# The expert stage's row loads issued from SyncE instead of ScalarE

## The reference

```python
x = x + tanh(g_xattn) * xattn(layernorm(x), ctx_512, ...)   # 16 heads, 375 context rows
x = x + tanh(g_ffn)   * ffn(layernorm(x), ...)

# ffn, N = 16 * 112 = 1792 tokens, E = 64 experts, H = 512, I = 128:
logits = x @ gate_w.T
topv, topi = top_k(logits, 8)
W = zeros((N, E)); W[n, topi[n]] = softmax(topv[n])
gate, up = split(einsum('nh,eih->nei', x, gu_w))
out = einsum('nei,ehi->nh', silu(gate) * up * W[:, :, None], dp_w)
out = out + sigmoid(x @ sh_gate1_w.T) * (silu(x @ sh_gate_w.T) * (x @ sh_up_w.T)) @ sh_down_w.T
```

## Time and profile before

| | |
|---|---|
| median of three runs | 1579.57 us |
| profiled execution, its time | 1578.49 us |
| profiled execution, span of the core | 1576.7 us |
| mean granted TensorE clock | 0.966 of full speed |
| busy: PE, PEld | 91%, 74% |
| busy: DVE, ACT, POOL | 72%, 43%, 50% |
| HBM traffic | 240 GB/s over the span |

### The profile page before, as it was taken

One profiled execution on the slowest core, in us unless ns is written; L12 is line 12 of the kernel. 1 busy time (PEld: TensorE's weight loads), 2 busy tenths in 40 slices (PEclk: granted clock), 3 DMA queues, 4 the chain that ended last, 5 costly groups with the idle time before them and its releaser, 6 DMA issues.

```text
span 1576.7 us, 24944 instructions
## 1 busy us (share of the span) xinstructions
PE 1430.7 (91%) x7674; PEld 1165.9 (74%) x7674; DVE 1140.1 (72%) x2601; ACT 671.6 (43%) x1558; POOL 784.4 (50%) x858
## 2 busy tenths in 40 slices
PE   6999799999899999989999999988299999999985
PEld 5766787777688777768777767867189999988742
DVE  5767684188788258779618887726388999988587
ACT  3332574011277011147501117703167777767521
POOL 4654573045577438777434787523524443333322
PEclk9999899999999999999999999998599999999998
DMA  7898993555596677730085764087799999999698
GB/s 243 293 318 280 288 299 95 194 170 182 179 285 203 218 242 245 231 103 17 28 274 185 234 195 149 3 287 247 220 311 331 330 359 370 369 339 348 203 429 343
DMA packets 164358, 380.08 MB, mean 241 GB/s; under 512 B 20200, under 2 KB 55682, under 8 KB 162434
## 3 DMA queue, kind: packets, MB, share of 16 engines
q1 hardware_dynamic: 136182, 286.33, 54.6%
q0 software_dynamic: 20608, 62.28, 11.5%
q10 hardware_dynamic: 7436, 29.88, 5.6%
HBM read 238.82 MB, written 139.59 MB: 240 GB/s over the span
## 4 chain that ended last, share of the span: by engine, by line
PE 60%; DVE 14%; DMA 11%; issue 7%; POOL 5%; ACT 2%; SPq 1%; POOLq 0%; DVEq 0%; ACTq 0%
PE bank L777 16%; PE bank L779 15%; PE bank L778 15%; PE bank L875 7%; PE bank L901 3%; DMA p_in<-parts 3%; DMA w_ex<-in_w_ex 3%; DVE q_sin L1190 2%; DMA parts<-y_sb,to_row 2%; PE bank L1040 2%; POOL q_rope L1846 2%; POOL slot_rows L1868 1%; DVE q_rope L1186 1%; POOL prob L1852 1%; DMA x_sb<-in_x 1%
## 5 line engine op out<-in xcount | busy, mean ns | idle before, releaser
L1846 POOL TENSOR_TENSOR q_rope<-q_rope,q_sin 128x448 f32<-128x448 f32 x192 | 217.7, 1162 | 157.6 <-DVE q_sin L1190 157.4
L1924 POOL DMA_INDIRECT parts<-y_sb,to_row x140 | 137.3, 981 | 220.7 <-ACT y_sb L1752 190.5
L1852 POOL TENSOR_TENSOR prob<-prob,row_inv 128x375 f32<-128x375 f32 x219 | 176.5, 812 | 103.6 <-DVE row_inv L1212 101.3
L875 PE MATMUL bank<-q_rope,m_w 128*128 128x448 f32 x384 | 159.7, 552 | 13.9 <-DVE q_tl L1196 10.4
L1190 DVE TENSOR_TENSOR q_sin<-bank,sin_q 128x448 f32<-128x448 f32 (+1 forms) x256 | 158.1, 617 | 4.0
L1868 POOL DMA_INDIRECT slot_rows<-rows,pos_i x112 | 110.0, 982 | 92.8 <-DVE count L1297 64.3
L1204 DVE TENSOR_REDUCE row_max<-bank 128x1 f32<-128x375 f32 x224 | 119.5, 534 | 39.7 <-PE bank L779 39.1
L901 PE MATMUL bank<-ident,prob 128*125 128x128 f32 x672 | 115.0, 282 | 21.8 <-POOL prob L1852 10.3
L1614 ACT ACTIVATE prob<-bank,row_max 128x375 f32<-128x375 f32 x224 | 128.3, 573 | 12.8 <-DVE row_max L1204 12.2
L901 PEld LDWEIGHTS bank<-ident,prob 128*125 128x125 f32 x672 | 103.3, 190 | 31.3 <-POOL prob L1852 20.9
L875 PEld LDWEIGHTS bank<-q_rope,m_w 128*128 128x128 f32 x384 | 71.9, 193 | 70.9 <-issue 65.9
(11 more groups left out here) (364 smaller groups left out, 4392.9 us busy)
## 6 DMA issues: line engine op xcount, KB each, us to landing
w_ex<-in_w_ex SPq DMA_DIRECT2D x64, 768.0 KB
slot_rows<-blank SPq DMA_DIRECT2D x64, 612.0 KB
p_in<-parts SPq DMA_DIRECT2D x14, 2048.0 KB, 16.8
m_w<-m_dram SPq DMA_DIRECT2D x48, 192.0 KB
x_g<-slot_rows ACTq DMA_DIRECT2D x16, 476.0 KB
wq_s0h<-wq_dram SPq DMA_DIRECT2D x24, 256.0 KB
wq_s0l<-wq_dram SPq DMA_DIRECT2D x24, 256.0 KB
wq_s1h<-wq_dram SPq DMA_DIRECT2D x24, 256.0 KB
```

The lines of the kernel that those rows point to most:

```text
L875: m = pe.matmul(bank[5][:, 0:GT], m_w[n % NW][:, c, :], q_rope[h % 2][:, c, :], start=(c == 0), stop=(c == QC - 1))
L1846: pool.tensor_tensor(o[:, c, :], o[:, c, :], q_sin[:, c, :], ALU.add).then_inc(s_radd, 1)
L1852: pool.tensor_tensor(prob[i][:], prob[i][:], row_inv[:, i:i + 1].to_broadcast([P, L]), ALU.mult)\
L1924: pool.indirect_dma_start(parts, bass.IndirectOffsetOnAxis(ap=to_row[x % NROW][0:size, t:t + 1], axis=0), y_sb[x % NY][t][0:size, :], None)\
```

## The change

`load_slots` moves from the shared helpers into `sync`, so that SP issues all 64 row loads. In SP's loop the row load for x + 5 stands ahead of the weight load for x + 3. ACT's loop has no row load any more, and ACT's wait for `s_order` in front of the stage goes as well; SP keeps its own.

```diff
-        def load_slots(eng, x):
-            e = eng.value_load(order[0:1, x:x + 1], min_val=0, max_val=E - 1)
-            size, n = TILES[x]
-            if x >= NXE:
-                eng.wait_ge(s_et, FIRST[x - NXE + 1])
-                eng.wait_ge(s_own, 3 * (x - NXE) + 1)
-            eng.dma_start(x_g[x % NXE][0:size, 0:n, :], ...).then_inc(s_xg[x % NXE], 16)
...
+            def load_slots(x):
+                e = sp.value_load(order[0:1, x:x + 1], min_val=0, max_val=E - 1)
+                size, n = TILES[x]
+                if x >= NXE:
+                    sp.wait_ge(s_et, FIRST[x - NXE + 1])
+                    sp.wait_ge(s_own, 3 * (x - NXE) + 1)
...
...
             for x in range(NXE):
-                load_slots(sp, x)
+                load_slots(x)
                 if 1 <= x + 1 < NE:
                     load_expert(x + 1)
             for x in range(E):
+                if x + NXE < E:
+                    load_slots(x + NXE)
                 if x + NE < E:
                     load_expert(x + NE)
                 if x in REST_AT:
                     load_base(EARLY_TILES + REST_AT.index(x))
...
             act.wait_ge(s_route, NR * B)
-            act.wait_ge(s_order, 1)
...
                 if x < E:
                     inner(x)
-                if x + NXE < E:
-                    load_slots(act, x + NXE)
                 if x >= 1:
                     down(x - 1)
```

More of the change, by code:

```diff
@@ L490, in behind_loop @@
                         body(eng, r, x)
-        def load_slots(eng, x):
-            e = eng.value_load(order[0:1, x:x + 1], min_val=0, max_val=E - 1)
-            size, n = TILES[x]
-            if x >= NXE:
-                eng.wait_ge(s_et, FIRST[x - NXE + 1])
-                eng.wait_ge(s_own, 3 * (x - NXE) + 1)
-            eng.dma_start(x_g[x % NXE][0:size, 0:n, :], slot_rows.rearrange("(e m) w -> e m w", m=SPAN)
-                         [bass.ds(e, 1), 0:size * n, :].rearrange("one (p t) w -> p (one t) w", t=n))\
-                .then_inc(s_xg[x % NXE], 16)
         def sync(sp):
@@ L730, in load_expert @@
                     .then_inc(s_ew[x % NE], 16)
+            def load_slots(x):
[4 more added lines that the diff above has]
+                    sp.wait_ge(s_own, 3 * (x - NXE) + 1)
+                sp.dma_start(x_g[x % NXE][0:size, 0:n, :], slot_rows.rearrange("(e m) w -> e m w", m=SPAN)
+                             [bass.ds(e, 1), 0:size * n, :].rearrange("one (p t) w -> p (one t) w", t=n))\
+                    .then_inc(s_xg[x % NXE], 16)
             for step, b in END:
```

## The result

| | before | after |
|---|---|---|
| median of 7 runs | 1579.57 us (1577.64 to 1584.17) | 1596.81 us (1592.99 to 1605.6) |
| profiled execution, time and span | 1578.49, 1576.7 us | 1599.24, 1597.4 us |
| mean granted TensorE clock | 0.966 | 0.964 |

The ratio is 1.0111, with 95% between 1.009 and 1.0133. The change makes the kernel slower by about 17 us. It was predicted at 1577.9 us, in a range up to 1588.

What follows compares the result with a forecast made beforehand. It took TensorE, VectorE and the full DMA engines to bound the expert stage. ACT -0.3, start +0.3, queues -1.5 and scatters -0.2 sum to -1.7 us, from 1579.57 to 1577.9 us; range 1571.5 to 1588.

Steps and rivals of the forecast that it cites:

- the queues' term: Rows and weights in one queue: weights land a little sooner; between -1.8 and +1.8 us, taken as -1.5.
- Rival A: At ACT's split of the next weights, rows ahead hold the weights up: 4.5 to 17.5 us, 1590.6 us; chance 0.21.
- Rival B: Waits for weights between 1380 and 1432 us go almost wholly: -7.5 us, 1572.1 us; chance 0.19.
- Rival C: One queue or two move the same bytes through full engines, so nothing changes: 1579.6 us; chance 0.21.
- The limit of 11.3 us: How long a weight load may take with three buffers at 4.8 us an expert: 3 x 4.8 - 3.10.
- ACT's part: Row loads leaving ACT gain 0 to 1.0 us, taken as 0.3, since idle time waiting for PE hides them.
- SP's part: SP has room for the row loads; the added wait delays no weight load in the steady loop: 0 us.
- The start: In the first turn, expert 5's rows travel ahead of expert 3's weights: 0 to 1.0 us lost, taken as 0.3.

Runs made afterwards that it cites:

- f4: Kernel before (two queues) with the row loads of all two-tile experts brought up to 128 rows, added rows unused: 1570.8 us, ratio 0.9924.
- f2: Changed kernel (one queue) with the row loads of all two-tile experts brought up to 128 rows, added rows unused: 1572.21 us, ratio 0.9945.
- e1: Changed kernel with SP's two issues swapped, weights ahead of rows, still one queue: 1596.46 us, ratio 1.0088.
- e2: Changed kernel with each row load issued by SP one expert later, still one queue: 1601.54 us, ratio 1.0129.
- e5: Kernel before with rows and weights of even experts issued by SP, of odd ones by ACT, both queues mixed: 1588.86 us, ratio 1.0049.
- e6: Changed kernel with row loads rounded up to a multiple of 16 rows, added rows unused: 1583.93 us, ratio 1.0015.
- f1: Changed kernel with two-tile row loads below 120 rows brought up to 120, added rows unused: 1608.41 us, ratio 1.0154.
- e4: Changed kernel with weight loads of experts 4 to 63 issued by ACT, rows left on SP, so two queues: 1581.33 us, ratio 1.0008.
- e11: e4 with row loads rounded up to a multiple of 16 rows: 1580.15 us, ratio 1.0000.
- e10: Changed kernel with 64 more tiny transfers on SP's queue, one per expert between rows and weights: 1599.86 us, ratio 1.0112.
- e12: Kernel before with 64 more tiny transfers on SP's queue, one per expert ahead of the weights: 1582.96 us, ratio 1.0021.
- f3: Kernel before with two-tile row loads below 120 rows brought up to 120, added rows unused: 1588.78 us, ratio 1.0035.

## Why the prediction was wrong

**The step that failed** is the queues' term. It said that "with the DMA full they take the same time in any order", bounded the term at -1.8 to +1.8 us and took -1.5. Measured, it is about +17 us, for the other terms leave next to nothing. The sentence treats a share near 1 as a fixed rate in bytes. Here such a share only says that packets were in flight; how long each one takes is open (2.77 to 3.63 us per MB in these runs). It went from 2.97 to 3.19 us per MB when rows and weights came into one queue. And the weights were to land a little sooner, or at most 1.8 us later; the loads of 1300 to 1380 us took 13.6 us instead of 9.3. In the chain between 1380 and 1432 they were to be one fewer or 0.5 us shorter; after has 14.03, 16.85 and 15.56 us there, where before had 13.13, 13.74 and 14.05.

What makes the price high is shown: the row counts of the loads. With row loads of 128 rows, one queue takes 0.9945 against 0.9924 of two, which the intervals do not tell apart; with the loads as they are it takes 1.0111 against 1. So the 17 us are a product of two things, row loads of fewer than 128 rows beside weights of 128, and one queue for both. Even in the kernel before these shapes cost about 12 us (f4), 7.2 of them in the stretch in which the prediction had read the loss as bytes of `load_base`.

**Rival A** had the place and the sign: ACT waits for weights already between 1260 and 1380, and 17.5 us was the upper end of its price. The way it gave is not enough. It blamed the rows ahead of the weights, but in f2 they stand ahead of them in the same order, with 12% more bytes, and the weights land after 6.9 us. Whether standing in line adds to the slower packets where the rows are as they are is not separated: in e1 and e2 the rows still stand ahead. A's slack was about 2 us, over the 1.5 from which it put its price at 4.5 us, so by its own reckoning it would have come to little more than that and not to 17. The argument against A, that "what rows take later they have left free earlier", was the same mistake about a full share. **Rival B** had said that the same bytes could move faster. f2 and f4 show that they can, though not by this change. **Rival C**, nothing at all, is what f2 and f4 show for loads of 128 rows.

**The limit of 11.3 us** for a weight load held: at 13.9 us a load the pace is 5.68 us an expert, which is (13.9 + 3.1) / 3.

**ACT's part** was read rightly. The issues are gone from ACT and no time came back for them; the wait for PE stood where the prediction put it (42 times still). In f2 and f4, where nothing else is short, moving the issues from ACT to SP changes 0.0021 (3 us) for the worse, inside the error. **SP's part** too: it waits ahead of each of 60 weight loads.

**The start** is a small loss at most. ACT's split of expert 3's weights is later than 1159.14 with idle time ahead of it, as written down:

```profile
1161.83 1.06 ACT L1735 ACTIVATE w_gu_s1h<-w_ex 128x1024 fp32r<-128x1024 f32 x1 [2.69 <-DMA w_ex<-in_w_ex]
```

This is 2.69 us of idle time, more than the bound of 1.0 us, but ACT catches up on part of it. From the first tanh to that of the 21st expert after takes 1.3 us more than before (116.7 against 115.4), and f2, with the same order of issue, 0.7 us more than f4 (116.8 against 116.1). That is about the upper end of the term, 1.0 us, read from single traces.

## What stays open

- Why these loads cost more in one queue than in two, by which way the row count lengthens the packets, and whether it is the row count itself or that it is unlike the weights' 128. e5 (1.0049) suggests that it grows with the mixing inside a queue. No run or view here tells the 16 DMA engines apart.
- Whether the trouble of 120, 112 and 104 rows is one or several. By the ratios, in one queue e6, which still has 24 loads of 112 rows, is 11 us slower than f2, and f1 with 44 of 120 rows is 33 us slower. Most of what after loses, it loses over the 16 experts of 112 rows: 91.2 us from tanh to tanh against 79.5 before, while the 12 of 120 rows take 63.2 against 59.6. But e6, whose row loads for these 16 are the same, takes 82.5 us. 112 and 96 rows were not tried by themselves.
- The 12 loads of three tiles of 96 rows were left as they are in all runs.
- e4 and e11 seem to be held back by ACT's waits for PE's transposes. What two exchanged queues would give without these was not tried.

## What to carry to other kernels

Where the DMA share is near 1, do not take GB/s as fixed: divide the queues' time by their bytes for each stretch, and try letting the large loads all write 128 partitions, even with rows that nobody uses. Loads of unlike partition counts that run at the same time were better kept in separate queues here. And that no wait stands in a trace says nothing on the slack: measure the loads from issue to landing. Before the change they took 9.3 us at a limit of 11.3, and 4.3 us more were enough to set the pace.

## What was not expected of the hardware

- Where the two kinds of load share the 16 DMA engines at a share near 1, 12% more bytes of rows made the stage faster: 29.88 MB in loads of 96 to 128 rows cost 2.97 us per MB with the weights, 33.36 MB in loads of 128 (and the twelve of 96) cost 2.80.
- Cutting a load of 128 partitions at partition 64 costs 51 us over 64 experts in one queue and 34 us in two; cutting it into even and odd partitions costs 1 us in each, inside the error (all by the ratios). The Trainium skill, "SBUF — State Buffer", section "Door 1: The DMA port swizzle", says that partitions 0 to 63 reach only half of the memory's 16 ports, and by its formula the even partitions reach them all. These four runs agree with it.
- One queue against two is worth 17 us with the same bytes, and 14 and 20 us with the issues in another order (e1, e2). The Trainium skill, "DMA: Bandwidth & Descriptors", section "Issuing engines are not separate DMA queues", says that issuing from several engines saves only sequencer time. With loads of 128 rows these runs agree (1572.21 and 1570.8 us); with loads of 96 to 128 rows as they are they do not (1596.81 and 1579.57 us), and the measurement decides.
- 64 additional transfers of 16 x 8 bytes in a queue whose engines show a share near 1 cost 0.0001 and 0.0021 of the time (e10, e12), neither clear of nothing.
- Issuing a load of 120 or 104 rows costs ACT more than one of 128, 112 or 96. In the kernel before the median issue takes 570 ns at 120 rows (12 loads) and 552 at 104 (8), but 340 at 128 and 323 at 112 and 96. ACT's 59 row loads in f3, of which 44 have 120 rows (shortest, median and longest in ns; first and last start):

```profile
L499 ACTq DMA_DIRECT2D x_g<-slot_rows x59: 323/569/593, 1151.0 to 1466.4; - x59
```

The same in f4, with 128 rows:

```profile
L499 ACTq DMA_DIRECT2D x_g<-slot_rows x59: 323/339/399, 1149.9 to 1449.8; - x59
```
